# A two-layer network in one launch: work moved across the seams between its blocks

## What is computed

```python
# layer 0
h = layernorm(x) * (1 + ca) + sa
x = x + ga * (chunked_recurrence(h @ W_aiv) @ W_mix + b_mix)      # 1024 channels
h = layernorm(x) * (1 + cb) + sb
x = x + gb * moe(h)         # 8 experts, 2 per row, and one shared; hidden size 512
# layer 1
h = layernorm(x) * (1 + ca) + sa
x = x + ga * windowed_attention(h)     # 16 query heads, 4 key heads, 128 rows to each side
h = layernorm(x) * (1 + cb) + sb
y = h
for l in range(2):
    q, k, v = split(shift_token(y) @ wqkv[l])                     # 8 heads of 64
    y = y + local_attention(rotary(l2norm(q)), rotary(l2norm(k)), v) @ wo[l]
    u = layernorm(shift_token(y)) * lg[l] + lb[l]
    a, g = split(u @ w1[l] + b1[l])                               # 682 + 682
    y = y + (a * gelu(g)) @ w2[l] + b2[l]
x = x + gb * y
```

## Time and profile before

| of the profiled execution | |
|---|---|
| its own time | 3396.15 us |
| span of the trace | 3394.4 us |
| mean granted TensorE clock | 0.963 of full speed |
| instructions | 45964 |
| TensorE busy | 3156.8 us, 93% of the span |
| VectorE busy | 1943.7 us, 57% |
| ScalarE busy | 1574.6 us, 46% |
| GpSimd busy | 700.6 us, 21% |

### The profile page before, as it was taken

The page is one execution under the profiler, slowest core; times in us unless marked ns, Lnnn a source line. Parts: engine busy times, 40 slices in busy tenths (PEclk is TensorE's granted clock), DMA queues, the critical chain, the costliest instruction groups (busy, mean ns, idle before and its releaser), DMA issues. The chain is left out here.

```text
span 3394.4 us, 45964 instructions
## 1 busy us (share of the span) xinstructions
PE 3156.8 (93%) x15106; PEld 1814.1 (53%) x15107; DVE 1943.7 (57%) x4736; ACT 1574.6 (46%) x3534; POOL 700.6 (21%) x837
## 2 busy tenths in 40 slices
PE   8899998989999979999969999997998999997998
PEld 4455555555666523333326666664555666664555
DVE  6999995541111156666647878773224777774332
ACT  5666652212222236666655666662123655654121
POOL 0000003550000045555432323220001111110111
PEclk9999999999999979999989999998999999998999
DMA  9800004012111111111011000000001000000000
GB/s 337 269 1 1 0 1 156 27 58 93 45 45 45 39 44 28 28 30 28 19 40 41 8 10 10 9 5 27 0 0 34 10 10 10 8 7 3 13 13 25
DMA packets 117579, 133.96 MB, mean 39 GB/s; under 512 B 14435, under 2 KB 104823, under 8 KB 117115
## 3 DMA queue, kind: packets, MB, share of 16 engines
q1 hardware_dynamic: 110794, 114.27, 10.3%
q0 software_dynamic: 6576, 17.05, 1.6%
HBM read 60.22 MB, written 60.83 MB: 36 GB/s over the span
## 5 line engine op out<-in xcount | busy, mean ns | idle before, releaser
L1709 DVE CUSTOM_DVE_ANT_0 sb_win_masked<-ps_win_pss,sb_win_around 128x384 f32<-128x384 f32 (+1 forms) x512 | 256.3, 537 | 178.3 <-PE ps_win_pss L1814 178.1
L2314 PE MATMUL ps_loc_psa<-sb_stk_w,sb_loc_hT 128*128 128x512 f32 x768 | 350.1, 606 | 5.2 <-DMA sb_stk_wo<-in_loc_wo 3.4
L2601 PE MATMUL ps_mlp_ps<-sb_mlp_hT,sb_stk_w 128*128 128x512 f32 (+1 forms) x768 | 324.2, 615 | 22.3 <-DVE sb_mlp_hid L2554 22.3
L2111 ACT ACTIVATE sb_loc_pr<-ps_loc_psw,sb_loc_nb,sb_loc_sc 128x256 f32<-128x256 f32 x512 | 281.0, 568 | 114.4 <-DVE sb_loc_nb L2239 114.4
L1814 PE MATMUL ps_win_pss<-sb_win_kT,sb_win_q 32*128 32x384 f32 (+1 forms) x1024 | 236.8, 534 | 38.1 <-DVE sb_win_qtok L1709 35.7
L1603 ACT ACTIVATE sb_win_pT<-ps_win_pst 128x512 f32<-128x512 f32 x368 | 199.8, 595 | 127.2 <-PE ps_win_pst L1825 125.3
L2554 DVE SCALAR_TENSOR_TENSOR sb_mlp_hid<-ps_mlp_ps,sb_stk_col,sb_mlp_gl 128x512 f32<-128x512 f32 x96 | 71.6, 749 | 305.0 <-ACT sb_mlp_gl L2523 305.0
L2523 ACT ACTIVATE sb_mlp_gl<-ps_mlp_ps,sb_stk_col 128x512 f32<-128x512 f32 x96 | 65.9, 687 | 383.4 <-PE ps_mlp_ps L2601 383.2
L2601 PEld LDWEIGHTS ps_mlp_ps<-sb_mlp_hT,sb_stk_w 128*128 128x128 f32 (+1 forms) x768 | 130.8, 184 | 202.6 <-issue 202.6
L2314 PEld LDWEIGHTS ps_loc_psa<-sb_stk_w,sb_loc_hT 128*128 128x128 f32 x768 | 142.0, 191 | 181.6 <-issue 177.8
L719 PE MATMUL ps_rec_psp<-sb_rec_hT,sb_rec_w 128*128 128x512 f32 x512 | 232.2, 597 | 0.8 <-DVE sb_keep_modf L476 0.8
(11 more groups left out here) (313 smaller groups left out, 6443.9 us busy)
## 6 DMA issues: line engine op xcount, KB each, us to landing
sorted_tokens<-sb_rec_blank SPq DMA_DIRECT2D x9, 4224.0 KB, 30.1
sb_exp_rows<-sorted_tokens SPq DMA_DIRECT2D x71, 128.0 KB, 2.0
expert_results<-sb_exp_res SPq DMA_DIRECT2D x71, 128.0 KB, 1.7
sb_moe_w_in<-in_L_ffn_w_in_eDF SPq DMA_DIRECT2D x8, 512.0 KB, 11.4
sb_moe_w_sw<-in_L_ffn_w_swiglu_eDF SPq DMA_DIRECT2D x8, 512.0 KB, 11.4
sb_exp_w_out<-in_L_ffn_w_out_eFD SPq DMA_DIRECT2D x8, 512.0 KB, 7.2
sb_win_sums<-sb_win_raw SPq DMA_DIRECT2D x128, 32.0 KB, 2.0
sb_stk_angles<-in_angles SPq DMA_DIRECT2D x32, 128.0 KB, 3.7
```

The source lines that it names most:

```text
L1709: nc.vector.tensor_tensor_reduce(masked[:, pair % 2, j, 0:keys], pss[:, (n + j) % PLAIN, 0:keys], around[:, first:first + keys], 1.0, -3e3 ...
L2111: e = nc.scalar.activation(pr[:, hf, h], psw[:, hf, h // 2, h % 2 * 256:h % 2 * 256 + 256], ACT.Exp, scale=sc8[:, b, hh:hh + 1], bias=nb[: ...
L2314: t = nc.tensor.matmul(psa[:, c], hT[:, b, k, 1 - k:P + 1 - k], w[:, k, c * 512:(c + 1) * 512], start=(k == 0), stop=(k == KD - 1))
L2601: i = nc.tensor.matmul(ps[at:at + M, q % 2, i2], w1[:, k, i2 * HID + f * P:i2 * HID + f * P + M], hT[:, b, k], start=(k == 0), stop=(k == ...
```

## The change

The lines of eight parts, in program order.

- **Recurrence to routing.** The routing norm's object, `moe_scale_row` and `moe_shift_row` live from the start of layer 0. Its statistics of the first group go ahead of `add_half(14)`, its `inverse_deviation` behind `mixed(14)` on ScalarE, and route's ScalarE loads no activation table. `scale_rows` stays behind the barrier.
- **Expert weights.** The nine `w_out` loads go from SyncE's queue, behind four row loads, to the head of GpSimd's; GpSimd also clears the semaphores of the new pool.
- **Windowed attention, start.** SyncE issues the local layer 0's weights and four loads of angles behind the block's own. `wog` is made at k = 6 of the first two steps; TensorE waits for it only in `project_out`.
- **Windowed attention, end.** The last tile's four copies of sums, and its four copies of `oT`, are split: lanes 0 and 1 by SyncE's queue, 2 and 3 by ScalarE's. The first three tiles' rows (tiles 0, 16 and 1) are normalised at s = 32 and 33 into `lead`, GpSimd issues the loads of the masks and does the three rows' modulation at the end.
- **Local layer.** The first three tiles read `lead`. GpSimd clears one column of `hT` and makes tables(0) before it clears `v` and `kT`; ScalarE waits only for the first, TensorE waits for all at its first scores. The reciprocals are copied into `oT` instead of `riT`.
- **Local layer to MLP.** The MLP norm's statistics of half 0 follow `add_output(28)`, those of half 1 `add_output(29)`, `scale_rows` of half 0 follows `add_output(30)`; `inverse_deviation` goes behind tile 30's moves; TensorE transposes half 0 in tile 31 ahead of its turns, ScalarE makes the affine step. The copies of tile 31 are issued by SyncE at the start of the MLP's block, and the wait for the copies moves to VectorE there. `scale_rows` of half 1 opens VectorE's list, its transposes come after `up(1)`, its affine step after the second gelu.
- **MLP, last rows.** `late` = y + b2 of the last 512 rows is made by GpSimd at the block's start; in L = 1 two more operations make x + gate * (y + b2) of it. The last `down` goes in two halves of two tiles, and VectorE's `finish` adds each half (in L = 1 after a product with the gate). SyncE stores each half for itself. `gate` of the half before goes behind `hid(11)`.
- **Gates** are stored in a buffer of three instead of four parts.

The core of the diff:

```diff
 # gated_recurrence, VectorE / ScalarE
                 columns(1, SHIFT_A, 2)
+                dve.wait_ge(s_x, 2 * (NBLK + 1))
+                keep["route_norm"].statistics(dve, 0)
                 add_half(2 * GROUPS - 2)
...
                     mixed(n)
+                    if n == 2 * GROUPS - 2:
+                        keep["route_norm"].inverse_deviation(act, 0)
 # route, ScalarE / VectorE
-                nc.scalar.preload_act_table_set(LN_SET)
-                norm.inverse_deviation(act, 0)
...
-                norm.normalise(dve, 0)
+                for b in range(NB):
+                    norm.scale_rows(dve, 0, b)
 # run_experts, GpSimd (the same three lines leave SyncE's list)
+                for e in range(EXP + 1):
+                    src = a["L0_ffn_w_out_eFD"][e] if e < EXP else a["shared_out"]
+                    pool.dma_start(w_out[:, e], src.rearrange("(k p) d -> p k d", p=P)).then_inc(s_wo, 16)
                 t["route"].clear_behind(pool)
 # windowed_attention, SyncE
                 sp.dma_start(around[:], a["win_around"]).then_inc(s_w, 16)
+                load_attention_weights(sp, a, S, 0)
+                for j in range(RING):
+                    sp.dma_start(S["angles"][:, j], a["angles"][:, j]).then_inc(S["loc"][f"angles_in{j}"], 16)
...
-                    for c in range(AKV):
+                    for c in lanes(u, 0):
 # GpSimd, at the block's end
+                for dst, name in ((S["mask"], "loc_mask"), (S["identb"], "ident")):
+                    pool.dma_start(dst[:], a[name]).then_inc(S["loc"]["masks_in"], 16)
+                for i in range(LEAD):
+                    b = i % NB
+                    pool.wait_ge(s_lxn, i + 1)
+                    nc.gpsimd.tensor_tensor(lead[:, i], lead[:, i], keep["scale_row"][:, b], ALU.mult).then_inc(s_lym, 1)
+                    pool.wait_ge(s_lym, i + 1)
+                    nc.gpsimd.tensor_tensor(lead[:, i], lead[:, i], keep["shift_row"][:, b], ALU.add
+                                            ).then_inc(S["loc"]["in"], 1)
 # ScalarE
+                        if k == 3 and s - 2 == NT - 1:
+                            act.wait_ge(s_logs, NT - 1)
+                            move_last_sums()
+                        if k == 6 and s == NT:
+                            lead_deviation()
+                        if k == 2 and s == NT + 1:
+                            lead_rows()
+                        if k == 7 and s == NT + 1:
+                            pack_last_output()
 # VectorE
+                        if k == 6 and s < 0:
+                            gate_output_weights(s + 2)
+                        if k == 5 and s == NT:
+                            lead_statistics()
+                        if k == 7 and s == NT:
+                            lead_offsets()
 # local_attention, SyncE
-                for i in range(TILES):
+                for i in range(TILES - 1):
...
-                sp.wait_ge(s_xs, (L + 1) * TILES * 32)
 # GpSimd
+                nc.gpsimd.memset(hT[:, :, 1, 0:1], 0.0).then_inc(s_pad, 1)
+                pool.wait_ge(s_k8, (L + 1) * 16)
+                tables(0)
                 nc.gpsimd.memset(v[:, :, 1], 0.0).then_inc(s_pad, 1)
                 nc.gpsimd.memset(kT[:, :, :, 1], 0.0).then_inc(s_pad, 1)
 # ScalarE
+                    if i == TILES - 2:
+                        norm.inverse_deviation(act, I0)
+                    if i == TILES - 1:
+                        act.wait_ge(S["mlp"]["w_in"], (L + 1) * 80)
+                        for k in range(KD):
+                            norm.affine_chunk(act, I0, 0, k, psa[:, k])
 # VectorE, behind add_output(i)
+                    if i == TILES - 4:
+                        dve.wait_ge(s_y, F + FIRST_UNITS + L + 1)
+                        dve.wait_ge(s_xs0, (L + 1) * FIRST_UNITS * 32)
+                        norm.statistics_of(dve, I0, 0, 0)
+                    if i == TILES - 3:
+                        norm.statistics_of(dve, I0, 1, 0)
+                    if i == TILES - 2:
+                        norm.scale_rows(dve, I0, 0, 0)
 # TensorE
+                    if i == TILES - 1:
+                        for k in range(KD):
+                            norm.turn(pe, I0, 0, k, psa[:, k], first=True)
                     turn(i, 0)
 # gated_mlp, SyncE
+                tail = y[:, NB * TPB - 1, P:D]
+                sp.dma_start(xs_b[1:P, NB - 1, TPB - 1], tail[0:P - 1]).then_inc(s_xs, 16)
+                sp.dma_start(xs_b[0:1, NB - 1, TPB], tail[P - 1:P]).then_inc(s_xs, 16)
...
+                    for h in range(2):
+                        sp.wait_ge(s_late, 4 + h + 1)
+                        sp.dma_start(out[:, late_rows(h)], late[:, 2 * h:2 * h + 2]).then_inc(s_store, 16)
 # GpSimd
+                nc.gpsimd.tensor_tensor(late[:], y[:, tiles(BLOCKS - 1)], b2[:].broadcast_to([P, TB, D]), ALU.add
+                                        ).then_inc(s_late, 1)
+                if LAST:
+                    pool.wait_ge(s_late, L + 1)
+                    nc.gpsimd.tensor_tensor(late[:], late[:], keep["gates"][:, 2, NB - 1:NB].broadcast_to([P, TB, D]), ALU.mult
+                                            ).then_inc(s_late, 1)
+                    pool.wait_ge(s_late, L + 2)
+                    nc.gpsimd.tensor_tensor(late[:], x[:, tiles(BLOCKS - 1)], late[:], ALU.add).then_inc(s_late, 1)
 # VectorE
+                dve.wait_ge(s_xs, (L + 1) * (TPB * NB - FIRST_UNITS) * 32)
+                norm.scale_rows(dve, I0, 1, 0)
 # finish(), for h in range(2), LAST
+                            nc.vector.tensor_tensor(g, part, keep["gates"][:, 2, NB - 1:NB].broadcast_to([P, TB // 2, D]),
+                                                    ALU.mult).then_inc(s_yo, 1)
+                            dve.wait_ge(s_yo, done + h + 1)
+                            nc.vector.tensor_tensor(late[:, 2 * h:2 * h + 2], g, late[:, 2 * h:2 * h + 2], ALU.add).then_inc(s_late, 1)
 # otherwise
+                            nc.vector.tensor_tensor(y[:, late_rows(h)], part, late[:, 2 * h:2 * h + 2], ALU.add).then_inc(s_yo, 1)
 # TensorE
                         up(q)
+                        if j == 0 and q == 1:
+                            turn(I0, 1)
...
+                            for h in range(2):
+                                products(b, range(2 * h, 2 * h + 2))
```

More of the change, by code:

```diff
@@ L152, in statistics, with statistics_of @@
             i.then_inc(self.s_mv, 1)
+    def statistics_of(self, dve, it, b, j):
+        nc = self.nc
+        for t in range(TB):
+            parts = self.halves(b, t, j)
+            for k, part in enumerate(parts):
+                i = nc.vector.bn_stats(self.stats[:, b, t, k], part)
+        i.then_inc(self.s_st, 1)
+        dve.wait_ge(self.s_st, it * NB + b + 1)
+        for t in range(TB):
+            i = nc.vector.bn_aggr(self.mv[:, b, t], self.stats[:, b, t, 0:len(self.halves(b, t, j))])
+        i.then_inc(self.s_mv, 1)
     def scale_rows(self, dve, it, b, j=None, ahead=False):
@@ L1750, in _ @@
                 offsets(0)
-                dve.wait_ge(s_w, 48)
-                for b in range(NB):
-                    nc.vector.tensor_tensor(wog[:, b], wo[:], keep["gates"][:, 1, 0, b:b + 1].broadcast_to([P, AG // 2, D]),
-                                            ALU.mult).then_inc(s_wog, 1)
                 combine(1)
@@ L2469, in gated_mlp, with late_rows @@
         BLOCKS = NBLK * NB
+        def late_rows(h):
+            first = tiles(BLOCKS - 1).start + h * (TB // 2)
+            return slice(first, first + TB // 2)
         def tiles(n):
@@ L2505, in affine @@
                         norm.affine_chunk(act, it, b, k, pst[:, k])
-                deviation(I0)
                 act.wait_ge(s_w, (L + 1) * 80)
-                for b in range(NB):
-                    affine(I0, b)
                 for j in range(NBLK):
@@ L2615, in down @@
                         i.then_inc(s_out, 1)
+                    def down(b):
+                        pe.wait_ge(s_hid, it * UF + (b + 1) * KH)
+                        if j or b:
+                            pe.wait_ge(s_yo, L * (BLOCKS + 1) + j * NB + b)
+                        if ahead or not b:
+                            products(b, range(TB))
+                        else:
+                            for h in range(2):
+                                products(b, range(2 * h, 2 * h + 2))
                     for q in range(UF):
                         up(q)
+                        if j == 0 and q == 1:
+                            turn(I0, 1)
                         if q == KH + 1:
@@ new lines, in attention_buffers @@
+def attention_buffers(nc, ctx, keep):
+    m = Pool(nc, ctx, "stk")
+    S = {
+        "pool": m,
+        "lead": m.sb("lead", [P, LEAD, D]),
+        "angles": m.sb("angles", [P, RING, 2, 2, LHD]),
+        "mask": m.sb("mask", [P, 3, 2 * P], BF16),
+        "identb": m.sb("identb", [P, P], BF16),
+        "w": m.sb("w", [P, KD, 3 * INNER]),
```

(13 more changed lines are left out.)

324 lines of the change are left out of this document (180 added, 144 removed).

## The result

The changed kernel took 3351.4 us (median of four runs, 3350.77 to 3353.89) beside 3394.44 us of the kernel before: a ratio of 0.9872, 95% interval 0.9855 to 0.9889. Forecast were 3357 us, with 3345 to 3370 around it. The span of its profile is 3350.1 us, 44.3 less than before; forecast were 37.2.

A forecast was written before the change was run, and what follows sets the result against it. TensorE, busy 93% of the span, was taken as the bound, so gains come only from its idle seams. Terms 2.8 + 4.2 - 1.0 + 9.2 + 6.4 + 4.8 + 4.0 + 6.8 = 37.2 us gave 3357, range 3345 to 3370.

The forecast's parts named there:

- if a steady loop changes its pace: Stated sign that the prediction is wrong, beside TensorE waiting for w_out beyond 3.5 us.
- less 1 for row loads that now share the rings: Expert weights: 1 us taken off the gain of 3.5 + 1.6 from w_out loads landing earlier.
- The transfers bind: Expert weights: if a load's issue costs about 1 us whatever its rows, transfers set the landing, 3.5 us earlier.
- Start of the windowed block: First transposes 0.75 us earlier by moving wog, gathers +1.8 beside local weights; loss 1.0, between gain 0.75 and loss 4.
- End of the windowed block, start of local layer 0: Split copies end the block 1.85 us earlier and the projection starts at 1773.8; together gain 9.2, between 7.5 and 10.5.
- Local to MLP: Layer 0 seam: half 0 ready ahead, no barrier wait for copies, inserted work costs 3.3; gain 6.4 us, between 2 and 10.
- Layer 1 of the same seam: Local to MLP in layer 1: VectorE held by GpSimd's late operations until 7.3 us; gain 4.0, between 1 and 10.
- MLP to local layer 1: Last add halved, input copy not waiting for memsets, projection 3.6 us earlier, 1.2 from clock; gain 4.8, between 3 and 5.5.
- the holes were worth more: Rival: low clock behind holes makes them worth more, and statistics may be covered; 3348 us, chance 0.14.
- New prices: Rival: shared transfers at the window's start 3 more, inserted statistics and lock 2.5 each; 3365 us, chance 0.10.
- the slower case: Rival: GpSimd's queue pays a price per 128 rows for the nine loads; at 2.0 us, 3416 us, chance 0.02.
- the loads issued by rows: Rival: GpSimd's issue time for w_out scales with rows, loss 5 us instead of gain 4.2; 3366, chance 0.12.

The follow-up runs named there:

- e9: The changed kernel run once more without any edit, as the measure for the run beside it: 3349.83 us.
- e7: Changed kernel, but in the last MLP block GpSimd makes the two further operations of late behind block 3 instead of at the start: 3373.81 us (one run, longer routing).
- e1: Changed kernel, but GpSimd waits until the first two row loads have landed before it issues the nine w_out loads: 3354.2 us.
- e2: Changed kernel, but the nine w_out loads are issued by SyncE behind four row loads, as in the kernel before: 3354.95 us (one run).
- e5: Changed kernel, but in both MLP blocks half 1 is transposed ahead of up(0) instead of behind up(1): 3399.66 us (one run, longer routing).
- e10: Changed kernel with local weights and angles issued behind windowed tiles 6 and 8 to 11, and late's two further operations behind block 3: 3343.22 us.
- e4: Changed kernel with the local layer's weights and angles issued later in the windowed block and wog made ahead of the first units again: 3351.94 us (one run).

## Why the prediction was right, and where it was wrong

- *What bounds the kernel.* Right: the work on TensorE stayed (15106 records) and most of the time came from seams; 7.1 of the 44.3 us are shorter busy time of TensorE. But "all steady loops keep their instructions, so I sum over the seams" left out that they don't keep their clock: routing gained 3.5 us, the windowed block lost 4.2 between its first transposes and the 60th score record. By the forecast's own sign, "if a steady loop changes its pace", this premise failed.
- *Recurrence to routing.* Right in each step: transposes 3.66 us earlier (3.7 forecast), a wait of 0.51 us for the shared weights, first product 2.7 earlier (2.8).
- *Expert weights.* Wrong: 4.2 us forecast, -0.3 measured. The step that failed is "less 1 for row loads that now share the rings": they took 7.4 instead of 2.1 us to land, and TensorE waited 5.4 us more for rows, which is what the missing wait for `w_out` (3.5) and the full clock behind it (1.6) gave. What the forecast took as the open question was no problem: GpSimd issues a load of 512 rows in 0.76 us (6.05 for eight), not by rows. "The transfers bind" was right; I then counted only one of the two that share them. The view of DMAs of this stretch:

```profile
sb_exp_w_out<-in_L_ffn_w_out_eFD POOLq DMA_DIRECT2D x8, 512.0 KB, 8.5
sb_exp_rows<-sorted_tokens SPq DMA_DIRECT2D x7, 128.0 KB, 7.4
sb_exp_w_out<-in_shared_out POOLq DMA_DIRECT2D x1, 512.0 KB, 13.1
```

- The estimate by the Trainium skill (DMA: Bandwidth & Descriptors, Anatomy of one DMA) had all nine loads landed 12.8 us behind their first issue; they took 19.1 (749.05 to 755.10 + 13.1), with row loads beside them, at some 350 GB/s. Here the measurement decides: that rate was not reached.
- *Start of the windowed block.* The sign was right and the size not: +1.8 was taken for the gathers, from 0 to 4.7, and it was 4.0 (5.09 against 1.06 us). "The gathers are issued first and one shares only its end" is what failed: GpSimd's first gather was issued at 1180.84, SyncE's first large load of the local layer at 1181.56, and VectorE needs the second gather too. With the 0.6 that `wog` gave, the transposes came 3.1 us later (16.82 against 13.68). Behind it came 4.2 us of low clock up to the 60th score record that the forecast had not; in e9 it was 1.4 for the same code, so most of this is not fixed by the change.
- *End of the windowed block, start of local layer 0.* Right in its parts: 1.87 us (1.85 forecast) and 7.36 (7.35).
- *Local to MLP.* The mechanism and nearly every time in it were right: block end, transposes of half 1, `up(2)`. With the lead that the changed kernel had at tile 25 added (8.8 us: 2187.39 against 2196.15), its `up(2)` at 2300.28 stands at 2309.0; forecast was 2309.3. The term that was mis-sized is where the kernel before had its `up(2)`: the forecast has "the ninth (`up(2)`) at 2316.7", that is, four records for each `up`. Each of its four products shows as two records, so `up(2)` is the seventeenth, at 2321.31 in that trace: 4.6 us more. The "1.0 for the low clock behind the idle" didn't come either: there is hardly an idle time left, the 16 records took 7.10 us at full clock (8.1 before), and the low clock behind the later hole was shorter as well (1.1 us). With 6.4 + 4.6 + 1.0 + 1.1 = 13.1 the sum is at the measured 13.3. The price of the inserted work, from tile 25's projection to the last output product, was 3.2 us (3.3 forecast).
- *Layer 1 of the same seam.* 12.5 us instead of 4.0. The same 4.6 of the misplaced `up(2)` is in it, and the inserted work cost 1.3 us there and not 3.3 (123.79 against 122.51 us). The lock was right in kind; as a hole it was half in size: 1.16 us more than in layer 0 (2.18 against 1.02) instead of 2.4. GpSimd's last operation ended 7.2 us behind the start, as forecast (7.3), but in layer 0 too VectorE began later than forecast, at 5.9 instead of 4.9 (2296.96, start 2291.03), as the copies landed then. e7 shows that with the clock it cost 3.5 us in all, more than the 2.4.
- *MLP to local layer 1.* 3.6 us came as forecast. The "1.2" for a clock that is not lowered did not: it was lowered as before (0.77 granted in both), and the 12 records took 6.99 us (7.00 before). And the last `down` in two halves took 11.21 instead of 10.82 us, a price that the forecast did not have.
- *End.* 6.6 us from the last product on (6.8 forecast).
- *Rivals.* The two MLP seams gave more, as in "the holes were worth more", but 4.6 us of it in each layer is the misplaced `up(2)` and not the rival's clock. "New prices" is what came at the windowed block. Neither the slower case nor the loads issued by rows came.
- *Sums.* 3.5 + 1.6 - 1 is 4.1 and not 4.2, and half of the bounds gives 3349 to 3370 instead of 3348 to 3367. Neither changes the forecast by more than 3 us.

## What to carry to other kernels

When a DMA is moved ahead of another, price both: here what was loaded early landed early at the cost of what shared the rings, and where all of it was needed at once none of the three orders gained more than 1.7 us. A load that is not needed for hundreds of microseconds does not belong beside a block's first gathers (4.6 to 4.9 us from moving it, against the runs beside it). Hold a run against runs of the same chip and time: stretches that no edit touched differ by 1 to 2 us from one chip to another. And before counting products in a trace, check with one group how many records a product leaves.

## What the runs showed of the hardware

- Behind a block's start the low clock can last long, and not equally long in the same code: from the experts' end to the 60th score record the granted clock averaged 0.56 over 70 us in the changed kernel and 0.62 over 67 us in e9, the same kernel. Up to the windowed block's last value product the kernels with this block unchanged (first profile, e1, e2, e5 to e9) took 576.8 to 579.9 us. Between the first profile and e9, 3.2 us of difference lie in this block (16.48 + 15.47 + 35.02 against 16.82 + 16.32 + 36.98 us), and at most 0.7 in any other stretch. So some 3 us at this place come and go with the same program.
- Stretches that no edit touches can differ by 1 to 2 us with the chip: local layer 1's last seven tiles took 99.0 us in the first profile and in e5 to e10 (chip 2), and 100.9 in e1 to e4 (chip 14); MLP 0 from `up(8)` to its last `up` 208.9 and 210.6 us; `up(0)` and `up(1)` of MLP 1 with the hole behind them, where no edit touches them, 10.2 and 11.0. In MLP 0's stretch it is busy time of TensorE, 199.9 and 201.6 us, at a granted clock of 0.99 and 0.98. That chip 2 and chip 14 are what divides them is the simplest reading; one chip of each kind is all that the runs have.
- The last `down` of MLP 0, 48 records, took 0.39 us longer in two halves (11.21 against 10.82). No run took this part alone.
